# Row maxima of causal attention: four query tiles' key range folded in half, with a rectified difference

## The reference

```
scores = einsum('bhtd,bhsd->bhts', q, k) * scale
scores = where(causal, -inf, scores)
attn = softmax(scores, axis=-1)
seq_out = einsum('bhts,bhsd->bhtd', attn, v)
...
x = x + 0.5 * ffn(layernorm(x))
x = x + attn(layernorm(x))
x = x + 0.5 * ffn(layernorm(x))
```

## Time and profile before

| | us |
|---|---|
| median of three runs | 1975.96 |
| span of the profiled execution (first to last instruction) | 1971.5 |
| what lies around the span, against the median | 4.5 |
| TensorE, VectorE, ScalarE, GpSimd busy | 1906.8, 1623.9, 1483.3, 916.0 |
| first fill of pass 1 | 727.6 |
| first exponential of pass 2 | 764.2 |
| last fill's maximum | 1117.4 |
| last exponential starts | 1158.9 |

### The profile page before, as it was taken

The page is one execution under the profiler, slowest core; times in us unless marked ns, Lnnn a source line. Parts: engine busy times, 40 slices in busy tenths (PEclk is TensorE's granted clock), DMA queues, the critical chain, the costliest instruction groups (busy, mean ns, idle before and its releaser), DMA issues. The chain is left out here.

```text
span 1971.5 us, 52907 instructions
## 1 busy us (share of the span) xinstructions
PE 1906.8 (97%) x18490; PEld 1129.9 (57%) x18490; DVE 1623.9 (82%) x5453; ACT 1483.3 (75%) x4089; POOL 916.0 (46%) x549
## 2 busy tenths in 40 slices
PE   7999999999999989999999999899999999999998
PEld 4777763577775343434434367437777646777743
DVE  6999964899994579999999769779999548999844
ACT  5999993799997253777777754469999837999962
POOL 2787860578781040000000046337878406787700
PEclk9999999999999997999999999999999999999999
DMA  6121220112120040111111000002212201121301
GB/s 188 43 48 43 48 60 6 35 43 49 42 66 23 6 152 28 41 42 42 42 42 43 19 5 2 2 21 47 49 43 47 55 6 42 42 49 42 70 12 43
DMA packets 76106, 85.08 MB, mean 43 GB/s; under 512 B 17139, under 2 KB 50499, under 8 KB 75715
## 3 DMA queue, kind: packets, MB, share of 16 engines
q1 hardware_dynamic: 75647, 81.68, 16.3%
q10 hardware_dynamic: 196, 0.02, 0.0%
HBM read 21.14 MB, written 8.39 MB: 15 GB/s over the span
## 5 line engine op out<-in xcount | busy, mean ns | idle before, releaser
L304 ACT ACTIVATE probs<-probs,negmax 128x128 f32<-128x128 f32 x1024 | 399.8, 396 | 23.2 <-DVE negmax L377 22.1
L2083 ACT ACTIVATE gprobs<-ps_global 128x1024 f32<-128x1024 f32 (+3 forms) x384 | 291.4, 810 | 124.3 <-PE ps_global L1548 101.2
L259 POOL TENSOR_TENSOR rot<-rot 128x1024 f32<-128x1024 f32 x128 | 302.5, 2363 | 145.6 <-DVE rot L347 145.6
L265 POOL TENSOR_TENSOR qk<-rot,cnorm 128x1024 f32<-128x1024 f32 x128 | 243.8, 1905 | 120.1 <-POOL rot L259 89.5
L272 POOL TENSOR_TENSOR probs<-probs,iden 128x1024 f32<-128x1024 f32 x128 | 242.9, 1898 | 120.0 <-DVE iden L385 120.0
L1778 DVE TENSOR_REDUCE maxes<-ps_global 128x1 f32<-128x512 f32 (+2 forms) x384 | 222.0, 637 | 10.2 <-PE ps_global L1511 6.5
L377 DVE CUSTOM_DVE_ANT_0 probs<-ps_attn,masks 128x128 f32<-128x128 f32 x1024 | 226.2, 285 | 0.0
L1506 PE MATMUL ps_global<-kq 48*128 48x512 bf16 (+3 forms) x768 | 196.7, 345 | 7.2 <-DVE maxes L1778 1.8
L304 ACT ACTIVATION_READ_ACCUMULATOR probs<-probs,negmax 128x1 f32 x1024 | 197.0, 192 | 0.0
L345 DVE TENSOR_TENSOR rot<-ps_attn,rotary 128x512 f32<-128x512 f32 x256 | 174.8, 683 | 1.8 <-PE ps_attn L171 1.6
L239 PEld LDWEIGHTS ps_attn<-probsT,v_first 128*64 128x64 f32 x2048 | 118.1, 136 | 98.1 <-ACT probsT L325 94.3
(11 more groups left out here) (212 smaller groups left out, 4585.0 us busy)
## 6 DMA issues: line engine op xcount, KB each, us to landing
v_first<-v_second SPq DMA_DIRECT2D x256, 128.0 KB, 2.3
hs<-z_a SPq DMA_DIRECT2D x256, 32.0 KB, 1.9
ln<-z_b SPq DMA_DIRECT2D x56, 128.0 KB, 2.4
kq<-split_scratch SPq DMA_DIRECT2D x64, 96.0 KB
kq<-split_scratch SPq DMA_DIRECT2D x64, 64.0 KB
split_scratch<-parts SPq DMA_DIRECT2D x8, 384.0 KB, 4.1
split_scratch<-gprobs SPq DMA_DIRECT2D x6, 384.0 KB, 3.9
x_tok<-in_x_dram SPq DMA_DIRECT2D x4, 512.0 KB, 6.4
```

Of the source, the lines that this page charges most:

```text
L259: nc.gpsimd.tensor_tensor(a, a, b, ALU.add).then_inc(C["rot_sum"], 1)
L265: nc.gpsimd.tensor_tensor(qk[:, k % 2, :].rearrange("p (h d) -> p h d", d=DH), rot_a[:, k % 2, :, :], cnorm[:, k % 2, :].unsqueeze(2).to_b ...
L304: last = nc.scalar.activation(probs[:, k % 2, slot, :], probs[:, k % 2, slot, :], ACT.Exp, scale=-1.0, bias=negmax[:, k % 2, slot:slot + 1 ...
L2083: nc.scalar.activation(probs[:, step % RING, 2 * p:2 * p + 2, 0:w], ps[:, S0 + 2 * p:S0 + 2 * p + 2, 0:w], ACT.Exp).then_inc(C["p2_exp"], 1)
```

## The change

Of tile 7 in every slot, of tiles 4 to 7 in slot 0 and of tiles 4, 5 and 7 in slot 1, the keys are folded in half. For a tile with 2w keys in sight, a fill of the kind GAP holds q times the second half of the keys, less q times the first half (a second matmul in the same 64-row half, whose weights are the negated queries, made on GpSimd by `negate`), with the causal mask added by the two small matmuls. ScalarE writes its rectified value to SBUF (`keep_gap`). A fill of the kind SUM holds q times the first half; VectorE adds the kept value to it and takes the maximum in one instruction of the form of L1774. A GAP fill gives VectorE nothing to do. GAP fills of tile 7 stand among tile 6's (or, in slots 0 and 1, those of tiles 4 to 7 among the fills of tiles 2 to 6); `FILLS_AT` stays. In slots 2 and up the order is now: 24 tile 6, 25 and 26 GAP, 27 and 28 tile 6, 29 and 30 GAP, 31 tile 6 (each 512 wide), 32 to 35 tile 6's other 384, 36 to 39 SUM. Slots 0 and 1 have 44 fills; 71 uses, not 63, come before the first exponential, and from there on the places are the same.

ScalarE runs `keep_gaps` for the fills that TensorE issued in the step before, between or behind the exponentials. One semaphore for each bank replaces `p1_free`. Kept values lie on a shelf of two halves; a GAP of tile 6 in slot 0 goes where that of tile 4 was and waits for VectorE's SUM of tile 4 (`KEPT_BEFORE`). GpSimd's memsets cover queries and keys, twice the columns.

```diff
+def p1_folded(t, kind):
+    half = (t + 1) * TILE // 2
+    return [(t, half if kind == GAP else 0, half, r, (p,), kind) for p in range(2) for r in range(2)]
+
+def in_turn(one, other):
+    other = [other[k ^ 1] for k in range(len(other))]
+    pairs = [pair if k % 2 == 0 else pair[::-1] for k, pair in enumerate(zip(one, other))]
+    return [fill for pair in pairs for fill in pair] + one[len(other):]
+
+def slot_fills(n):
+    short = p1_fills(0) + p1_fills(1)
+    if n >= 2:
+        return (short + sum((p1_fills(t) for t in range(2, 6)), []) + in_turn(p1_fills(6), p1_folded(7, GAP)) + p1_folded(7, SUM))
+    begun = short + in_turn(p1_fills(2), p1_folded(4, GAP)) + in_turn(p1_fills(3), p1_folded(5, GAP))
+    if n == 1:
+        return begun + p1_folded(4, SUM) + p1_folded(5, SUM) + in_turn(p1_fills(6), p1_folded(7, GAP)) + p1_folded(7, SUM)
+    return (begun + in_turn(p1_folded(4, SUM), p1_folded(6, GAP)) + in_turn(p1_folded(5, SUM), p1_folded(7, GAP)) +
+            p1_folded(6, SUM) + p1_folded(7, SUM))
...
+KEPT_BEFORE = {(0, 6): ((0, 4),), (0, 7): ((0, 5),), (1, 4): ((0, 6),), (1, 5): ((0, 7),), (1, 7): ((1, 5),), (2, 7): ((1, 4),),
+               (3, 7): ((1, 7),), **{(n, 7): ((n - 2, 7),) for n in range(4, SLOTS)}}
...
             def fill(n, f):
...
-                    pe.wait_ge(C["p1_free"], C.after("p1_free", use - RING + 1))
+                    await_release(pe, use - RING)
+                if kind == GAP:
+                    pe.wait_ge(C["p1_negated"], C.after("p1_negated", NEGATED.index((n, t)) + 1))
...
-                masked_here = on_diagonal(P1_FILLS[f]) and len(both) == 2
+                masked_here = on_diagonal(FILLS[n][f]) and (len(both) == 2 or kind == GAP)
...
+                    if kind == GAP:
+                        nc.tensor.matmul(out, negated[rows, NEGATED_AT[n, t], p, :], ks[buf][rows, p, 0:w],
+                                         start=False, stop=False, skip_group_check=True)
...
             def take_max(n, f):
...
+                if kind == SUM:
+                    await_release(dve, partner(n, f))
+                    nc.vector.tensor_tensor_reduce(bank, bank, kept(n, t, r, p0)[:, 0:w], 1.0, LEAST, ALU.add, ALU.max,
+                                                   maxes[:, n % 2, r, p0, t, c:c + 1]).then_inc(released(use), 1)
...
         @block.gpsimd
...
-            nc.gpsimd.memset(ks[RING - 1], 1.0).then_inc(C["pj_ones"], 1)
+            nc.gpsimd.memset(kq[:, RING - 1, :, :].bitcast(BF16), 1.0).then_inc(C["pj_ones"], 1)
...
+            def negate(n, t):
+                gp.wait_ge(C[f"qk_in{n % RING}"], C.after(f"qk_in{n % RING}", 16 * QK_DMAS * (n // RING + 1)))
...
+                nc.gpsimd.tensor_scalar(negated[:, at, :, :], qs[n % RING][:, :, tile_cols(t)], -1.0, None, ALU.mult
+                                        ).then_inc(C["p1_negated"], 1)
+
+            for n, t in NEGATED[0:6]:
+                negate(n, t)
+            split_max(0)
...
             def exp(n, u):
...
+                    if step >= 1:
+                        for part in ((0,), (1, 2))[p]:
+                            keep_gaps(uses_after(*before, part))
+
+            def keep_gap(n, f):
+                t, first, w, r, both, kind = FILLS[n][f]
+                use = p1_use(n, f)
+                act.wait_ge(C["p1_filled"], C.after("p1_filled", use + 1))
+                for m, g in KEPT_BEFORE.get((n, t), ()):
+                    await_release(act, p1_use(m, FILLS[m].index((g, 0, (g + 1) * TILE // 2, r, both, SUM))))
+                nc.scalar.activation(kept(n, t, r, both[0])[:, 0:w], ps[:, bank_of(use), 0:w], ACT.Relu
+                                     ).then_inc(released(use), 1)
```

More of the change, by code:

```diff
@@ L1247, in written_count, with p1_fills @@
     return 16 * 2 * (m // DEEP + 1)
-def p1_fills():
+PLAIN, GAP, SUM = range(3)
+def p1_fills(t):
     fills = []
[L1253 to L1259, removed]
-    return fills
-P1_FILLS = p1_fills()
-FILLS = len(P1_FILLS)
+    for first in range(0, (t + 1) * TILE, CHUNK):
+        w = min(CHUNK, (t + 1) * TILE - first)
+        pairs = ((0, 1),) if 2 * w <= CHUNK else ((0,), (1,))
+        fills += [(t, first, w, r, both, PLAIN) for both in pairs for r in range(2)]
+    return fills
+def p1_folded(t, kind):
[14 more added lines that the diff above has]
+            p1_folded(6, SUM) + p1_folded(7, SUM))
+FILLS = [slot_fills(n) for n in range(SLOTS)]
 TURN_AFTER = 2
+NEGATED = [(0, 4), (0, 5), (0, 6), (0, 7), (1, 4), (1, 5), (1, 7)] + [(n, 7) for n in range(2, SLOTS)]
+NEGATED_AT = {use: (k if k < 6 else k % 2) for k, use in enumerate(NEGATED)}
 P2_UNITS = ([(0, s, s * TILE) for s in range(4)] + [(1, s, CHUNK) for s in range(4)] +
@@ L1495, in fill @@
             def fill(n, f):
-                t, c, w, r, both = P1_FILLS[f]
+                t, first, w, r, both, kind = FILLS[n][f]
                 use, buf = p1_use(n, f), n % RING
@@ L1573, in line_items @@
                 if n == 0:
-                    pe.wait_ge(C["p1_free"], C.after("p1_free", USES))
+                    for use in range(USES - RING, USES):
+                        await_release(pe, use)
                 if n == 2 * ITEMS:
@@ L1707, in _ @@
             wait(pe, "ln_out", CHUNKS)
-            for use in range(FILLS + AHEAD):
+            for use in range(USES_BEFORE):
                 produce(use)
@@ L2080, in exp @@
                     act.wait_ge(C["p2_av"], C.after("p2_av", step - RING + 1))
+                before = divmod(step - 1, U2)
                 for p in range(2):
@@ L2084, in exp, with keep_gaps @@
                                          ACT.Exp).then_inc(C["p2_exp"], 1)
+                    if step >= 1:
+                        for part in ((0,), (1, 2))[p]:
+                            keep_gaps(uses_after(*before, part))
+            def keep_gap(n, f):
+                t, first, w, r, both, kind = FILLS[n][f]
+                use = p1_use(n, f)
[3 more added lines that the diff above has]
+                nc.scalar.activation(kept(n, t, r, both[0])[:, 0:w], ps[:, bank_of(use), 0:w], ACT.Relu
+                                     ).then_inc(released(use), 1)
+            def keep_gaps(uses):
+                for use in uses:
+                    n, f = use_of(use)
+                    if f is not None and FILLS[n][f][-1] == GAP:
+                        keep_gap(n, f)
             def copy_out(n, c):
@@ L2206, in _ @@
                 copy_values(m)
-            for m in range(CHUNKS - DEEP, CHUNKS):
+            for m in (DEEP, DEEP + 1):
+                act.wait_ge(C[f"pj_written{m % DEEP}"], C.after(f"pj_written{m % DEEP}", written_count(m)))
+            keep_gaps(range(USES_BEFORE))
+            for m in (DEEP - 2, DEEP - 1, DEEP + 2):
                 act.wait_ge(C[f"pj_written{m % DEEP}"], C.after(f"pj_written{m % DEEP}", written_count(m)))
```

96 lines of the change are left out of this document (61 added, 35 removed).

## The result

The changed kernel takes 2017.35 us (median of four runs, 2015.81 to 2020.59) against 1976.70 of the kernel before beside it: 1.0209 times as long, 95% interval 1.0195 to 1.0224. It is slower by 41 us; 2008 was forecast, with 1990 to 2026 as the forecast's own range.

A forecast was written before the change was run, and what follows sets the result against it. VectorE looked busiest (97%), but TensorE was taken as the chain from fill 24 to 31, VectorE again behind it. Steady slots +24.8 and start +7 gave 32 us on 1976: 2008 us, own range 1990 to 2026.

The forecast's parts named there:

- A steady slot, +1.65: Slots 0 to 14: TensorE's and ScalarE's added work delays the slot's last maximum, 1.65 us a slot, +24.8 us in all.
- a pair costs 1.05 us in place of 0.22: Two adjacent GAP fills on TensorE run one after the other, adding 0.8 us twice a slot.
- ScalarE's part: Steady slot: rectifying fills 29 and 30 delays the exponentials of step 4, so VectorE stands 0.5 us more.
- Saved where it had to wait anyway: Steady slot: VectorE's 2.4 us of dropped reductions fall where it had to wait anyway.
- The start, +7: Ahead of the first exponential: three waits of 4.2, 5 and 8 us against 9.9 us less VectorE work; bounds -10 to +14.
- The waits: At the start, VectorE runs dry: +4.2 for the negation, +5 in mixed GAP groups, +8 for shelf places.
- The shelf: Slot 0: rectifications of tiles 6 and 7 wait for SUMs of tiles 4 and 5 to leave their places, +8 us.
- the negation: Start: the first GAP waits for GpSimd's longer memset and then the negated queries, +4.2 us.
- that rival: ScalarE: rectifier outside the exponential's table set, each group costing two table loads, 77 us more, 2085; chance 0.02.
- The faster rival: VectorE stays fed in the steady slots, -2.4 us each: 1940, or 1958 with half of it; chance 0.17.
- that of no change: GAPs partly overlap neighbours of the other half, giving back 1.6 us a slot, and the start breaks even: 1976; chance 0.06.
- The one of bare rectifications and a low clock: Step 4's exponentials wait for both whole pairs, 2.8 us a slot, plus 14 at the start: 2032; chance 0.05.

The follow-up runs named there:

- narrow: The changed kernel, but from the fifth slot on each rectification takes 32 columns of its bank instead of 512; 2000.12 us.
- both_light: The changed kernel without a GAP's negated-query product and mask products, and with rectifications of 32 instead of 512 columns from the fifth slot on; 1984.75 us.
- placed: The changed kernel folding only tile 7, slot 0's negation ahead of the third memset, fill order and `FILLS_AT` counts chosen anew from the second slot on; 1969.73 us.
- plain_placed: The kernel before, without any fold, with its 40 fills in another order and other `FILLS_AT` counts, chosen the same way; 1960.93 us.

## Why the prediction was right

The direction and the place came out of the mechanism that the prediction gave: the saved reductions stand where VectorE waits anyway, and the GAPs lengthen TensorE's and ScalarE's path to the next plain fills. The size, 2017 against 2008 and within the own range, owes something to luck: two errors in a steady slot nearly cancelled. Step by step:

- *A steady slot, +1.65*: +1.54 at full clock. The path to it was partly wrong. Counted from the transposition, fill 24 starts at 12.95 us (12.91 before): nothing changes up to there, as said. Fills 27 and 28 come 0.36 late (0.81 forecast), fill 31 comes 1.14 late (1.75), the last maximum 1.57 (1.66).
- *The step that failed: "a pair costs 1.05 us in place of 0.22"*, because the second GAP "cannot start before the first has issued". The rows show both first products at 915.51 and both negated ones at 915.73: the halves worked side by side and the pair cost 0.22 + 0.22 + 0.06 + 0.03 = 0.52. TensorE's added 1.6 us was 0.6, and taking it away gave 0.3. The trace of the kernel before had this already, right behind the earlier trace rows; the last section shows the rows.
- *ScalarE's part was put too low*: 0.5 us of the 1.65 for two late rectifications. Shortening all four gave 1.1. The bank was overlooked: a GAP holds one of three until ScalarE comes to it, and fill 32 waits for that (0.53 us in the row at 920.06). The two errors nearly cancelled, so the sum of the slot was right by luck, with a wrong split. No run takes the bank apart from the rectification's own time.
- *"Saved where it had to wait anyway"* held: with both costs small the saving of 2.3 us still bought 0.2.
- *The clock* was not in the sum of the steady slots. Seven stretches at the lower level cost 9.9 us of the profiled execution; before there were none. Less that, the profiled execution's 2020.59 would be 2010.7, against the 2008 of the forecast.
- *The start, +7*: +8.5 up to the first transposition, +9.1 up to the first exponential (776.02 us, 764.20 before, less the 2.7 ahead of pass 1), and the first slot +3.9 with its low clock (the half level holds from 734 to 782 us, before from 731 to 769). The waits were forecast at 17 us (4.2 + 5 + 8) and came to 14.3; VectorE's work was to fall by 9.9 and fell by 5.8 up to the transposition. The shelf, forecast at 8 us, gave back 4.6, and the negation, forecast at 4.2, gave back 1.35, alone and together. The wait for the transfers out of `parts` was put at nothing: the prediction doesn't name it.
- *No weight load shows*: the negated weights load from 915.51, while the first product of the same half runs, and the negated product starts 0.22 after it. As in the earlier trace rows, and against the rule of the Trainium skill ("TensorE: Matmul & The Clock Gate", "Part 3: Packing small matmuls — row/col tiling") that the prediction cited.
- *No table load*: in the rows above two rectifications take 1.08 us and exponentials follow them at once, and between 689 and 1286 us the trace has no table load, so that rival falls. The faster rival falls with VectorE at 81%, that of no change with the time. The one of bare rectifications and a low clock (2032) was half there: the row at 920.38 starts behind two whole rectifications, but the low clock that was not forecast came in the first slot and in the steady ones.

## What to carry to other kernels

Taking work off the busiest engine gains only where that engine ends last; find the stretch where it already waits, and see whether the saved instructions stand there. When an order is written out by hand for certain durations, a change of what each place feeds needs the order chosen again, and then the old work needs the same choice as a control: here the old work in a new order gained 14.5 us (1975.43, 1960.93), and the folded work in its own new order stayed 8.8 us behind that.

## What the hardware showed that was not expected

TensorE did not start these matmuls in program order. The order is product, negated product, two masks for one half, then the same for the other; the second half's first product starts at 915.51 with the first half's, 0.22 us ahead of the first half's negated product. The Trainium skill ("PSUM — Partial Sum Buffer", "Engine vs sequencer instructions") says that matmuls start and complete in program order; this trace disagrees for matmuls in different 64-row halves. So does that of the kernel before, right behind the fill of the earlier trace rows:

```profile
900.62 0.28 PE L1506 MATMUL ps_global<-kq 48*128 48x256 bf16 x2
...
900.74 0.22 PE L1509 MATMUL ps_global<-causal_sb 64*128 64x128 bf16 x2
...
900.80 0.19 PE L1511 MATMUL ps_global<-causal_sb 64*128 64x64 bf16 x2
```

One of each two belongs to the other p of that fill, the other to the next fill, in the opposite half: the next fill's first product starts at 900.62, ahead of the last two mask products of the fill before it (900.74, 900.80). The sentence ahead of the prediction that every engine takes its instructions in program order does not hold for TensorE, then; within one half the rows keep the order.

The granted clock fell to its lower level (1.2 of 2.4 GHz) inside some steady slots of kernels whose slots take 25.4 to 25.7 us, and each time cost 1.4 us; where it did not fall, TensorE was busy 24.93 of 26 us (the window from 905 to 931). In none of the slots of 24.6 us and less (narrow and both_light from their fifth slot, placed, plain_placed, before) did it fall. If the added waiting is what brought it down, that waiting was paid twice; that it is the cause, no run shows.
